# A slot schedule with two turned-back groups moved, one small result copied sooner, and two Vector steps written in fewer instructions

## The chip, the cores and the metric

The kernel runs on one core of a Trainium2 chip. The metric is the device time of one launch in microseconds; the time of a kernel is the median of its runs. Engines are named as the profile names them: PE is TensorE, PEld its weight loads, ACT is ScalarE, DVE is VectorE, POOL is GpSimd and SP is the queue that issues the transfers.

## The reference, cut to what matters

The model is two metaformer layers on an image batch of shape 8 x 96 x 128 x 128. Only the first layer's mixer and the first feed-forward matter here; the second layer is a convolution stage and another feed-forward. Cut down, the mixer is:

```python
feat, value = conv1x1(x, f_w, f_b), conv1x1(x, v_w, v_b)      # 4 heads of 24 channels, 4 quadrants of 64x64 tokens
ctr, value_centers = pool(feat), pool(value)                  # M = 4 centres for each head and quadrant
sim = sigmoid(beta + alpha * l2norm(ctr) @ l2norm(pts).T)     # 4 x 4096 for each head and quadrant
idx = argmax(sim, axis=1)                                     # each token keeps its best centre only, the first on a tie
sim = sim * (arange(M)[None, :, None] == idx[:, None, :])
agg = (sim @ value2 + value_centers) / (sum(sim, -1) + 1.0)
out = agg.T @ sim                                             # back to the tokens, then conv1x1 with proj_w
x = x + out
t = t + ffn(layernorm(t))                                     # hidden 384, operands rounded to an 8-bit float
```

## The kernel before, in words

The program has three phases, one after the other: `phase_a` (the mixer, the first feed-forward and the normalisation for the second layer, about 1,960 us), `phase_b` (the convolution over rows and columns) and `phase_c` (pointwise mix, gate and the second feed-forward). The change touches `phase_a` alone, and adds four columns to the constants.

**Steps and slots.** The image is cut into 32 quadrants of 4096 tokens (8 groups of 512 tokens, a group being `TPC` = 4 tiles of 128). `phase_a` is a software pipeline over quadrants. In step i each engine works on quadrant i (feed-forward), i+1 (result of the mixer, first norm of the feed-forward), i+2 (similarities) , i+3 (centres) and i+4 (turning the input). A step has nine slots, s = 0 to 8, written out by hand in the dictionaries at the top (`BIG_AT`, `FWD_AT`, `OUT_AT`, `COS_AT`, `SIM_AT`, ...); each of PE, ACT and DVE runs its own list through the slots, in program order, and waits on semaphores. POOL has its own order in a step (L1260 on), without slots.

What matters in a slot:

- The feed-forward of group s: PE `pe_hidden` in three parts j = 0, 1, 2 into two PSUM banks (L357), ACT `act_hidden` copies each (L370, tile `A_h`), DVE `dve_hidden` adds the bias and rounds (three L378, then one L382). ACT may run at most two groups ahead of DVE. PE `pe_q8` turns the next group's input (L267), ACT `act_q8` copies it (L305). `pe_y` (L297), `act_y` (L327) and `dve_y` (L249, L253) are group s-1.
- `big` (slots 0 to 3, two groups in each): features and dot products, PE L690, ACT L873 and L874; DVE `norms` reduces them (L1007), and after the fourth group of a half writes a seed (L1016) from which POOL computes inverse norms (`inverse_norms`, L1245 to L1258, result `A_rn`).
- `cosines` (slots 3 and 5, first DVE work of the slot) waits for `A_rn` of its half (L1025, L1029); then ACT takes the sigmoid (L956) and `similarity` (slots 4 and 6, last DVE work of the slot) finds the maximum (L1039), marks it (L1041), breaks ties (L1045, L1048, L1050) and writes the masked product (L1052). POOL `scaled_sim` (L1225) waits for that.
- The third stage of the output, x3: ACT `norm3` normalises a group (four L894; groups 0 to 3 in slots 7 and 8, groups 4 and 5 in slot 2 and 6 and 7 in slot 3 of the next step, `NORM3_LATE`). It waits for the shift that POOL `ln3` writes (L1207). PE `c_turn` turns a group back to channels (four L789 in a bank of the ring `back`), ACT `c_out` copies it out (L905), and SP stores a half when its four groups are there.
- The mixer's small chain for quadrant i+1: `gather_out` (slot 8), PE `sum_rows` (L729, L730), DVE `sum_out` (L1066), PE `values` (L738, first in slot 1, behind `keep_going`: matmuls on constants whose result nobody reads, L698), DVE `own_heads` (L1071, first in slot 1), PE `project` (slot 2), DVE `projected` (L1077, L1081), PE `out` (L781, slots 3 to 6).

PSUM banks are given out in rings: `front` with four banks, `back` with two. The order of the uses in a ring is the list written in the loop over slots, and a use waits for the reader of the use that had its bank before.

POOL's order in a step: the last half of `ln1` for i+3, `pool_norm` (L220, L229) of two groups, `ln3(p, 1)` for quadrant i-1 (p), `inverse_norms` of half 0, `pool_norm`, `inverse_norms` of half 1, `ln3(i, 0)`, `scaled_sim` of half 0, `ln2`, `centres`, `pool_norm`, `scaled_sim` of half 1, `ln2`, `pool_norm`, `ln1` for i+4.

Of the kernel before, what the change touches and what calls it, by code (L numbers as in the profile page):

```python
# [5 lines left out]
F32 = mybir.dt.float32  # L6
# [5 lines left out]
ALU = mybir.AluOpType  # L12
# [40 lines left out]
K_QUARTERS = K_ROWS + HM  # L53
K_W = K_QUARTERS + M

# [374 lines left out]
AGG_AT, SUM_AT, VAL_AT, PA_AT = 8, 0, 1, 2  # L430
KEEP_SIM, KEEP_VALUES = (8, 20), 12
NORM3_AT, NORM3_LATE = {7: (0, 1), 8: (2, 3)}, {2: (4, 5), 3: (6, 7)}


def phase_a(nc, consts, x, wf_t, wf, bf, wv_t, bv, wp_t, bp, alpha, beta, w1, b1, w2, b2, gamma, beta_ln, dw13, strip_dram, edge_dram, x2_dram, x3_dram):
# [4 lines left out]
    with ExitStack() as ctx:  # L440
# [3 lines left out]
        for s in range(FFN_SLOTS):  # L444
# [11 lines left out]
            if s == SUM_AT:  # L456
                front_uses.append(("sum", 0, 1, "summed", 0))
            if s == PA_AT:
# [3 lines left out]
            if s == AGG_AT:  # L462
# [190 lines left out]
        def _(pe):  # L653
# [138 lines left out]
            def body(i):  # L792
                q1, q2, q3, q4, p = i + 1, i + 2, i + 3, i + 4, i - 1
                for s in range(FFN_SLOTS):
# [27 lines left out]
                    if q1.real and s == SUM_AT:  # L822
                        sum_rows(i)
                    if q1.real and s == PA_AT:
# [142 lines left out]
        def _(dve):  # L967
# [63 lines left out]

            def similarity(q, h):
                n = NT // 2
                t, u = slice(h * n, (h + 1) * n), slice(h * n * HEADS, (h + 1) * n * HEADS)
                s3 = sim[:, t, :].rearrange("p t (h m) -> p (t h) m", m=M)
                e = eq[:, u, :]

                dve.wait_ge(ev["sig"], ev.at("sig", q, h))
                dve.tensor_reduce(mx[:, u], s3, AX_X, ALU.max).then_inc(ev["mx"], 1)  # L1039
                dve.wait_ge(ev["mx"], ev.at("mx", q, h))  # L1040
                dve.tensor_tensor(e, s3, mx[:, u].unsqueeze(2).to_broadcast([P, n * HEADS, M]),  # L1041
                                  ALU.is_equal).then_inc(ev["eq"], 1)

                dve.wait_ge(ev["eq"], ev.at("eq", q, h))
                dve.tensor_copy(taken[:, u, 0], e[:, :, 0]).then_inc(ev["tie"], 1)  # L1045
                for m in range(1, M - 1):
                    dve.wait_ge(ev["tie"], ev.at("tie", q, (M - 1) * h + m - 1))
                    dve.tensor_tensor(taken[:, u, m], taken[:, u, m - 1], e[:, :, m], ALU.max).then_inc(ev["tie"], 1)  # L1048
                dve.wait_ge(ev["tie"], ev.at("tie", q, (M - 1) * h + M - 2))
                dve.tensor_tensor(e[:, :, 1:M], e[:, :, 1:M], taken[:, u, :], ALU.is_gt).then_inc(ev["only"], 1)  # L1050
                dve.wait_ge(ev["only"], ev.at("only", q, h))
                dve.tensor_tensor(sim32[:, t, 0:HM], sim[:, t, :], e.rearrange("p (t h) m -> p t (h m)", h=HEADS),  # L1052
                                  ALU.mult).then_inc(ev["sim"], 1)

# [19 lines left out]
            def projected(q):  # L1074
# [45 lines left out]
            def body(i):  # L1120
# [3 lines left out]
                for s in range(FFN_SLOTS):  # L1124
# [851 lines left out]
```

## Time and profile before

| what | us |
|---|---|
| median of 3 runs (3660.05 to 3663.72) | 3662.53 |
| the profiled execution, its own time | 3659.49 |
| its span in the trace | 3657.6 |
| DVE busy over the span (88%) | 3218.4 |
| PE busy (82%) | 3017.4 |
| ACT busy (76%) | 2781.3 |
| POOL busy (47%) | 1728.9 |

The busy share of an engine is a mean over three phases with different limits, so it is read phase by phase. In a timeline of the trace a row gives the start, the time that the row's instructions cover, the engine and line, and in brackets how long the engine had stood idle before it and which instruction ended that. Rows that follow each other closely on one line are merged, with their count as x3.

### The profile page before, as it was taken

To read this page: it belongs to the slowest core of one execution; us is meant where nothing else is said; L and a number is where in the kernel's file an instruction comes from. 1 tells how busy PE (TensorE), PEld (TensorE's weight loads), DVE (VectorE), ACT (ScalarE), POOL (GpSimd) and SP (SyncE) were. 2 spreads that over 40 slices of the span, in tenths; PEclk is the share of its full clock that TensorE was granted. 3 is DMA by queue.
4 is the path that set the end of the run, shared out by engine and by line. 5 is a ranking of instruction groups with operands and counts; after the bars stand their busy time and mean duration, and the time that the engine had idled before them with its cause. 6 is when DMAs were issued, how large, how long until landed. Compare 5 with 4: busy or idle time off the path is not lost. (4 is left out here: it accounts for less than half of the span.)

```text
span 3657.6 us, 68122 instructions
## 1 busy us (share of the span) xinstructions
PE 3017.4 (82%) x21990; PEld 1910.0 (52%) x21990; DVE 3218.4 (88%) x8131; ACT 2781.3 (76%) x6274; POOL 1728.9 (47%) x2404
## 2 busy tenths in 40 slices
PE   6787888878787878887876799997888888888887
PEld 5565665656565656565654344443444444444444
DVE  4888889898989898989886699999899999999998
ACT  2577777777777877777778455554799999999998
POOL 3777777777787877787864000000222222222221
PEclk9999999899999999999987899999999999999999
DMA  3233323232323232323212888897676667666762
GB/s 68 53 89 74 91 71 88 71 88 70 88 71 88 71 88 71 88 71 88 71 56 69 212 238 234 236 280 212 172 199 188 181 185 200 184 184 193 199 177 83
DMA packets 696178, 478.92 MB, mean 131 GB/s; under 512 B 407217, under 2 KB 674422, under 8 KB 683830
## 3 DMA queue, kind: packets, MB, share of 16 engines
q1 hardware_dynamic: 695830, 474.58, 49.2%
q8 instruction: 182, 2.98, 0.3%
q14 instruction: 166, 1.36, 0.1%
HBM read 272.09 MB, written 201.92 MB: 130 GB/s over the span
## 5 line engine op out<-in xcount | busy, mean ns | idle before, releaser
L1891 POOL TENSOR_SCALAR C_var<-C_st 128x16 f32<-128x16 f32 x64 | 13.5, 211 | 1338.6 <-DVE C_st L178 1338.6
L1464 DVE SCALAR_TENSOR_TENSOR B_y<-B_mid,B_coefs,B_y 128x512 f32<-128x512 f32 x768 | 509.0, 750 | 3.2 <-ACT B_y L1429 3.2
L1395 PE MATMUL B_ps_row<-B_z,B_band 128*128 128x512 f32 x1152 | 499.1, 596 | 15.1 <-DMA B_band<-edge_scratch 15.1
L378 DVE TENSOR_SCALAR A_hq<-A_h,A_b 128x512 f16<-128x512 f16 x768 | 319.4, 456 | 176.5 <-ACT A_h L370 169.6
L370 ACT ACTIVATE A_h<-A_hid 128x512 f16<-128x512 f32 x768 | 428.3, 594 | 59.5 <-PE A_hid L357 57.1
L178 DVE BATCH_NORM_STATS2 A_st<-A_xT 128x6 f32<-128x192 f32 x1536 | 443.6, 349 | 29.3 <-ACT A_xT L861 16.0
L370 ACT ACTIVATE C_h<-C_hid 128x512 f16<-128x512 f32 x768 | 425.0, 589 | 22.9 <-PE C_hid L357 22.5
L1504 ACT ACTIVATE C_q<-C_xT,C_shift,C_rstd 128x96 fp8e5<-128x96 f32 x1024 | 392.6, 457 | 43.3 <-POOL C_shift L1898 43.2
L894 ACT ACTIVATE A_xc<-A_xT,A_shift,A_rstd 128x96 f32<-128x96 f32 x1024 | 379.3, 456 | 4.2 <-POOL A_shift L1207 4.0
L167 POOL TENSOR_TENSOR A_rstd<-A_var,A_expo 128x16 f32<-128x16 f32 x128 | 376.5, 2941 | 10.7
L1395 PEld LDWEIGHTS B_ps_row<-B_z,B_band 128*128 128x128 f32 x1152 | 218.8, 190 | 294.2 <-issue 287.8
L1738 PE MATMUL C_fbank<-C_y3q,C_pw 96*96 96x512 f32 x512 | 279.1, 627 | 77.7 <-DVE C_gated L1822 53.5
L357 PE MATMUL C_hid<-C_q8c,C_w 96*128 96x512 bf16 x768 | 259.3, 385 | 86.7 <-ACT C_h L370 83.4
L1420 ACT ACTIVATE B_mid<-B_ps_row,B_row_bias 128x512 f32<-128x512 f32 x192 | 130.4, 689 | 250.4 <-DVE B_y L1464 184.2
L297 PE MATMUL A_bbank<-A_w,A_hq 128*128 128x96 f16 x3072 | 192.6, 218 | 136.1 <-DVE A_hq L382 77.3
L357 PE MATMUL A_hid<-A_q8c,A_w 96*128 96x512 bf16 x768 | 267.3, 402 | 41.9 <-ACT A_h L370 39.5
L690 PEld LDWEIGHTS A_fbank<-A_big_w,A_xq 97*128 97x128 f32 x2048 | 275.9, 201 | 44.2 <-DVE A_pabd L1081 26.5
L690 PE MATMUL A_fbank<-A_big_w,A_xq 97*128 97x112 f32 x2048 | 282.2, 284 | 19.0 <-DVE A_pabd L1081 17.4
L378 DVE TENSOR_SCALAR C_hq<-C_h,C_b 128x512 f16<-128x512 f16 x768 | 243.7, 348 | 49.0 <-ACT C_h L370 38.9
L781 PE MATMUL A_fbank<-A_pabd,A_simT 128*128 128x384 f32 x512 | 244.0, 608 | 33.6 <-DVE A_xT L1088 33.6
L297 PEld LDWEIGHTS A_bbank<-A_w,A_hq 128*128 128x128 f16 x3072 | 165.5, 105 | 191.5 <-DVE A_hq L382 114.5
L305 ACT ACTIVATE A_q8c<-A_bbank 96x512 bf16<-96x512 f32 x256 | 149.3, 583 | 107.9 <-PE A_bbank L267 106.6
(167 smaller groups left out, 7248.7 us busy)
## 6 DMA issues: line engine op xcount, KB each, us to landing
A_xq<-in_x SPq DMA_DIRECT2D x32, 1536.0 KB, 8.9
x_scratch<-A_xT SPq DMA_DIRECT2D x64, 768.0 KB, 3.2
x_scratch<-A_x3h SPq DMA_DIRECT2D x64, 768.0 KB, 5.4
B_z<-x_scratch SPq DMA_DIRECT2D x96, 512.0 KB
y_scratch<-B_y SPq DMA_DIRECT2D x96, 512.0 KB, 3.6
C_x3q<-x_scratch SPq DMA_DIRECT2D x32, 1536.0 KB, 9.1
C_xT<-x_scratch SPq DMA_DIRECT2D x64, 768.0 KB, 16.6
C_y3q<-y_scratch SPq DMA_DIRECT2D x31, 1536.0 KB, 15.6
```

The source lines that it names most:

```text
L167: m = pool.tensor_tensor(rstd[:, o:o + n], var[:], expo[:, 0:n], ALU.pow)
L178: return dve.bn_stats(st[:, n:n + 2, :].rearrange("p t s -> p (t s)"), x[:, n * C:(n + 2) * C].rearrange("p (t c) -> p c t", t=2))
L297: m = pe.matmul(bank[:, t * C:(t + 1) * C], self.hq[:, b, s:s + P], self.w["w2"][:, j, :], start=(j == 0), stop=(j == NJ - 1))
L357: pe.matmul(self.hid2[n % 2][:], self.w["w1"][:, j * P:(j + 1) * P], self.q8c[:, k % 2, :], start=True, stop=True).then_inc(ev["hidden"], 1)
L370: act.activation(self.h16[:, k % 2, j * CH:(j + 1) * CH], self.hid2[n % 2][:], ACT.Copy).then_inc(ev["h16"], 1)
L378: r = dve.tensor_scalar(self.hq[:, b, s], self.h16[:, b, s], self.w["b1"][:, j:j + 1], 0.0, ALU.add, ALU.max)
L690: m = pe.matmul(bank[:, t * BIGN:(t + 1) * BIGN], xq[q.buf(NX)][:, n * P:(n + 1) * P], big_w[:, :], start=True, stop=True)
L894: m = act.activation(xc3[:, k // 4, t % (NT // 2), :], xT[u.buf(NB)][:, t * C:(t + 1) * C], ACT.Identity, scale=rstd3[:, t:t + 1], bias=sh ...
L1395: m = pe.matmul(bank(c, h), band[c.buf(NB)][:, d, :], z[c.buf(NB)][:, half(h), d:d + W], start=(d == 0), stop=(d == 2))
L1464: dve.scalar_tensor_tensor(y, mid[c.buf(2)][:, half(h), t:t + W], coefs[:, c.n, 3 + t:4 + t], y, ALU.mult, ALU.add).then_inc(ev["sums"], 1)
L1504: m = act.activation(self.q8[:, t, :], x[:, t * C:(t + 1) * C], ACT.Identity, scale=self.rstd[:, t:t + 1], bias=self.shift[:, t:t + 1], sa ...
L1738: pe.matmul(rows(front.bank("pw", k)[0:C, 0:CH]), pw[:], flipped(y3q[q.buf(2)], k), start=True, stop=True).then_inc(ev["pw_full"], 1)
```

## The change

It does six things, all in `phase_a`:

1. `c_turn` and `c_out` of groups 2 and 3 of the previous quadrant move from slot 0 to slot 3.
2. `sum_rows` on PE moves from the end of slot 0 to a place ahead of the second `big` of slot 0, and its place in the `front` ring with it; `sum_out` on DVE moves from the end of slot 0 to right behind `dve_hidden`.
3. The matmuls nobody reads in front of `values` go from 12 to 3 (`KEEP_VALUES`).
4. The tie break uses the first mark itself, where it had been copied first (L1045), and keeps its running maxima in the same tile, whose rows are 9 elements long, not 4.
5. The masked product L1052 is written with its heads and centres as two dimensions, since the marks no longer lie together.
6. The projected block matrix is written by one instruction of 128 x 384 with a mask of own blocks, where there were four of 32 x 96.

```diff
-C_AT_BEFORE = {0: (2, 3), 4: (4, 5), 5: (6, 7)}
+C_AT_BEFORE = {3: (2, 3), 4: (4, 5), 5: (6, 7)}
...
-KEEP_SIM, KEEP_VALUES = (8, 20), 12
+KEEP_SIM, KEEP_VALUES = (8, 20), 3
...
-            front_uses += [("big", c, 2, "big", c) for c in BIG_AT.get(s, ())]
+            front_uses += [("big", c, 2, "big", c) for c in BIG_AT.get(s, ())[:1]]
+            if s == SUM_AT:
+                front_uses.append(("sum", 0, 1, "summed", 0))
+            front_uses += [("big", c, 2, "big", c) for c in BIG_AT.get(s, ())[1:]]
...
-        eq = sb("A_eq", [P, NT * HEADS, M], F32)
-        taken = sb("A_taken", [P, NT * HEADS, M - 1], F32)
+        eq = sb("A_eq", [P, NT * HEADS, M * (M - 2) + 1], F32)
...
                     if i.real and s < NK:
                         ff.pe_hidden(pe, i, s, 2)
+                    if q1.real and s == SUM_AT:
+                        sum_rows(i)
                     for c in bigs[1:]:
                         big(i, c)
...
-                dve.tensor_copy(taken[:, u, 0], e[:, :, 0]).then_inc(ev["tie"], 1)
                 for m in range(1, M - 1):
...
-                    dve.tensor_tensor(taken[:, u, m], taken[:, u, m - 1], e[:, :, m], ALU.max).then_inc(ev["tie"], 1)
...
+                    dve.tensor_tensor(eq[:, u, M * m], eq[:, u, M * (m - 1)], e[:, :, m], ALU.max).then_inc(ev["tie"], 1)
...
+                dve.tensor_tensor(e[:, :, 1:M], e[:, :, 1:M], eq[:, u, 0:M * (M - 2) + 1:M], ALU.is_gt).then_inc(ev["only"], 1)
...
-                for t in range(TPC):
-                    g = slice(32 * t, 32 * t + 32)
-                    m = dve.tensor_scalar(pabd[g, t * C:(t + 1) * C], s_pa[g, 0:C], rden[g, :], None, ALU.mult)
-                m.then_inc(ev["pabd"], 1)
+                dve.scalar_tensor_tensor(pabd[:].rearrange("p (t c) -> p t c", c=C),
+                                         s_pa[:, 0:C].unsqueeze(1).to_broadcast([P, TPC, C]), rden[:],
+                                         own_block.unsqueeze(2).to_broadcast([P, TPC, C]),
+                                         ALU.mult, ALU.mult).then_inc(ev["pabd"], 1)
...
                     if i.real and s < NK:
                         ff.dve_hidden(dve, i, s)
+                    if q1.real and s == SUM_AT:
+                        sum_out(q1)
```

## Rows read from the trace of the kernel before

**Rows 1.** The page, its first line.
```profile
span 3657.6 us, 68122 instructions
```
**Rows 2.** Busy time by windows, first phase: start:end, length, engines, clock, DMA.
```profile
300.00:1800.00 1500.00, 1221.21 (x12187) 910.83 (x12186) 1313.86 (x3684) 1153.37 (x2787) 1155.00 (x1670) 0.93 0.33 80
```
**Rows 3.** Line L1066 in 300 to 1800 us: durations, first and last start.
```profile
L1066 DVE COPY A_summed<-A_fbank x25: 162/165/167, 305.5 to 1751.2; 97x16 f32<-97x16 f32 x25
```
**Rows 4.** Waits in 300 to 1800 us: total us, times, longest.
```profile
DVE A_hq L378 <- ACT A_h L370: 122.4, 101, 2.7
...
DVE A_rn L1025 <- POOL A_rn L1258: 3.8, 10, 0.4
```
**Rows 5.** Timeline of DVE, slots 0 and 1 of one step.
```profile
1026.37 0.35 DVE L378 TENSOR_SCALAR A_hq<-A_h,A_b 128x512 f16<-128x512 f16 x1 [1.94 <-ACT A_h L370]
...
1030.12 1.19 DVE L378 TENSOR_SCALAR A_hq<-A_h,A_b 128x512 f16<-128x512 f16 x2 [1.14 <-ACT A_h L370]
```
**Rows 6.** Timeline of POOL, from the scaled similarities to the inverse norms.
```profile
1013.37 0.66 POOL L1225 TENSOR_TENSOR A_simr<-A_sim,A_rstd 128x256 f32<-128x256 f32 x1 [3.07 <-DVE A_sim L1052]
...
1035.86 0.22 POOL L1207 TENSOR_TENSOR A_shift<-A_less,A_rstd 128x16 f32<-128x16 f32 x1
...
1040.98 0.32 POOL L1258 TENSOR_TENSOR A_rn<-A_newton 128x64 f32<-128x64 f32 x1
```
**Rows 7.** Timeline of DVE, end of slot 2 and start of slot 3.
```profile
1039.64 1.30 DVE L1081 TENSOR_SCALAR A_pabd<-A_fbank,A_rden 32x96 f32<-32x96 f32 x4
1041.33 0.23 DVE L1025 TENSOR_TENSOR A_rn<-A_rn,A_guard 128x64 f32<-128x64 f32 x1 [0.39 <-POOL A_rn L1258]
```
**Rows 8.** Timeline of DVE, the tie break in slot 6, this step and the next.
```profile
1011.60 0.22 DVE L1045 COPY A_taken<-A_eq 128x64 f32<-128x64 f32 x1
1011.85 0.59 DVE L1048 TENSOR_TENSOR A_taken<-A_taken,A_eq 128x64 f32<-128x64 f32 x2
...
1072.74 0.42 DVE L1052 TENSOR_TENSOR A_sim<-A_sim,A_eq 128x256 f32<-128x256 f32 x1
```
**Rows 9.** Timeline of ACT, slot 0 (a pair of L905 and what follows), then slots 2 to 4.
```profile
1023.92 1.44 ACT L905 ACTIVATE A_x3h<-A_bbank,A_gb 96x512 f32<-96x512 f32 x2
1025.25 0.49 ACT L873 ACTIVATE A_sq<-A_fbank 128x384 f32<-128x384 f32 x1
...
1036.12 2.97 ACT L894 ACTIVATE A_xc<-A_xT,A_shift,A_rstd 128x96 f32<-128x96 f32 x8 [0.34 <-POOL A_shift L1207]
...
1042.18 0.49 ACT L873 ACTIVATE A_sq<-A_fbank 128x384 f32<-128x384 f32 x1 [0.43 <-PE A_fbank L690]
...
1043.08 2.96 ACT L894 ACTIVATE A_xc<-A_xT,A_shift,A_rstd 128x96 f32<-128x96 f32 x8
...
1050.37 0.60 ACT L370 ACTIVATE A_h<-A_hid 128x512 f16<-128x512 f32 x1 [1.06 <-PE A_hid L357]
```
**Rows 10.** Timeline of PE: matmuls on constants, later its waits in slot 4.
```profile
1026.06 2.11 PE L698 MATMUL A_fbank<-A_w,A_idb 96*128 96x384 bf16 x12
...
1040.38 0.39 PE L357 MATMUL A_hid<-A_q8c,A_w 96*128 96x512 bf16 x1 [1.27 <-ACT A_h L370]
...
1047.16 0.71 PE L789 MATMUL A_bbank<-A_cst,A_xc 128*96 128x128 f32 x4 [1.92 <-ACT A_q8c L305]
```
**Rows 11.** Line L1464, the nearest instruction of the new kind.
```profile
L1464 DVE SCALAR_TENSOR_TENSOR B_y<-B_mid,B_coefs,B_y x768: 744/749/756, 2046.2 to 2554.4; 128x512 f32<-128x512 f32 x192
```
**Rows 12.** Timeline of DVE, slot 4, in both steps.
```profile
1050.63 1.04 DVE L378 TENSOR_SCALAR A_hq<-A_h,A_b 128x512 f16<-128x512 f16 x3
...
1112.43 0.35 DVE L378 TENSOR_SCALAR A_hq<-A_h,A_b 128x512 f16<-128x512 f16 x1 [1.17 <-ACT A_h L370]
```
**Rows 13.** Timeline of ACT, slots 3 and 4 one step later.
```profile
1105.17 2.96 ACT L894 ACTIVATE A_xc<-A_xT,A_shift,A_rstd 128x96 f32<-128x96 f32 x8
...
1111.80 0.60 ACT L370 ACTIVATE A_h<-A_hid 128x512 f16<-128x512 f32 x1 [0.40 <-PE A_hid L357]
```
**Rows 14.** Busy time by windows, slot 4 of the same step.
```profile
1048.00:1054.00 6.00, 5.22 (x25) 3.58 (x26) 5.87 (x18) 2.69 (x5) 3.54 (x12) 0.50 0.58 104
```

More of the change, by code:

```diff
@@ L53 @@
 K_QUARTERS = K_ROWS + HM
-K_W = K_QUARTERS + M
+K_BLOCK = K_QUARTERS + M
+K_W = K_BLOCK + TPC
 class Events:
@@ L452, in phase_a @@
                 front_uses.append(("val", 0, 1, "aT4", 0))
-            front_uses += [("big", c, 2, "big", c) for c in BIG_AT.get(s, ())]
+            front_uses += [("big", c, 2, "big", c) for c in BIG_AT.get(s, ())[:1]]
+            if s == SUM_AT:
+                front_uses.append(("sum", 0, 1, "summed", 0))
+            front_uses += [("big", c, 2, "big", c) for c in BIG_AT.get(s, ())[1:]]
             front_uses += [("out", k, 1, "x1", k) for k in OUT_AT.get(s, ())]
             front_uses += [("fwd", k, 4, "xT", k) for k in FWD_AT.get(s, ())]
-            if s == SUM_AT:
-                front_uses.append(("sum", 0, 1, "summed", 0))
             if s == PA_AT:
@@ L472, in phase_a @@
                     c16=1, cw=1, cwc=1, big=NK, n2=NK, n2c=2, seed=2, rn_s=22, rn=2, guarded=2, cos=2, sig=2, mx=2, eq=2,
-                    tie=6, only=2, sim=2, simr=2, simT=2, side=1, sided=1, pool=1, agg=1, gathered=2, sum=1, summed=1, val=1,
+                    tie=2 * (M - 2), only=2, sim=2, simr=2, simT=2, side=1, sided=1, pool=1, agg=1, gathered=2, sum=1, summed=1, val=1,
                     rden=1, aT4=1, pa=1, pabd=1, bn3=NK,
@@ L495, in phase_a @@
         sel_quarters = cst[:, K_QUARTERS:K_QUARTERS + M]
+        own_block = cst[:, K_BLOCK:K_BLOCK + TPC]
         w_raw = sb("A_w_raw", [C, 2 * C], F32)
@@ L821, in body @@
                             fwd(i, k)
-                    if q1.real and s == SUM_AT:
-                        sum_rows(i)
                     if q1.real and s == PA_AT:
@@ L1035, in similarity @@
                 s3 = sim[:, t, :].rearrange("p t (h m) -> p (t h) m", m=M)
-                e = eq[:, u, :]
+                e = eq[:, u, 0:M]
                 dve.wait_ge(ev["sig"], ev.at("sig", q, h))
@@ L1044, in similarity @@
                 dve.wait_ge(ev["eq"], ev.at("eq", q, h))
-                dve.tensor_copy(taken[:, u, 0], e[:, :, 0]).then_inc(ev["tie"], 1)
                 for m in range(1, M - 1):
-                    dve.wait_ge(ev["tie"], ev.at("tie", q, (M - 1) * h + m - 1))
-                    dve.tensor_tensor(taken[:, u, m], taken[:, u, m - 1], e[:, :, m], ALU.max).then_inc(ev["tie"], 1)
-                dve.wait_ge(ev["tie"], ev.at("tie", q, (M - 1) * h + M - 2))
-                dve.tensor_tensor(e[:, :, 1:M], e[:, :, 1:M], taken[:, u, :], ALU.is_gt).then_inc(ev["only"], 1)
+                    if m > 1:
+                        dve.wait_ge(ev["tie"], ev.at("tie", q, (M - 2) * h + m - 2))
+                    dve.tensor_tensor(eq[:, u, M * m], eq[:, u, M * (m - 1)], e[:, :, m], ALU.max).then_inc(ev["tie"], 1)
+                dve.wait_ge(ev["tie"], ev.at("tie", q, (M - 2) * h + M - 3))
+                dve.tensor_tensor(e[:, :, 1:M], e[:, :, 1:M], eq[:, u, 0:M * (M - 2) + 1:M], ALU.is_gt).then_inc(ev["only"], 1)
                 dve.wait_ge(ev["only"], ev.at("only", q, h))
-                dve.tensor_tensor(sim32[:, t, 0:HM], sim[:, t, :], e.rearrange("p (t h) m -> p t (h m)", h=HEADS),
-                                  ALU.mult).then_inc(ev["sim"], 1)
+                dve.tensor_tensor(sim32[:, t, 0:HM].rearrange("p t (h m) -> p t h m", m=M),
+                                  sim[:, t, :].rearrange("p t (h m) -> p t h m", m=M),
+                                  e.rearrange("p (t h) m -> p t h m", h=HEADS), ALU.mult).then_inc(ev["sim"], 1)
             def gather_out(q):
@@ L1154, in body @@
                         gather_out(q2)
-                    if q1.real and s == SUM_AT:
-                        sum_out(q1)
                     if q3.real and s == MEAN_AT:
@@ L1945 @@
         consts[32 * t:32 * t + M, K_QUARTERS:K_QUARTERS + M] = np.eye(M, dtype=np.float32) / np.float32(2 * CH)
+    for t in range(TPC):
+        consts[32 * t:32 * t + 32, K_BLOCK + t] = 1
     consts[0:C, K_CEN:K_CEN + C] = np.eye(C, dtype=np.float32) - np.float32(1 / C)
```

## The prediction, made before the changed kernel ran

> **What bounds the kernel now.** I read the page first: the profiled execution has a span of 3657.6 us [rows 1]. The change touches only the first phase, so everything is read there. In the busy time by windows, 300 to 1800 us, DVE works 1313.9 of 1500 us (88%) and no other engine over 82% [rows 2]. So DVE looks like the bound, with 186 us left over. The period of a step is the spacing of a line that runs once in it: L1066 runs 25 times, first at 305.5, last at 1751.2, so (1751.2 - 305.5) / 24 = 60.24 us [rows 3]. The waits say what DVE lacks: 122.4 us are for ACT's copy of the hidden layer, 4.9 us a step, and only 3.8 us for POOL's inverse norms, but those ten times [rows 4]. The timeline puts the waits for ACT mostly into slots 0 and 1: 1.94 us before the last L378 of slot 0, 1.14 us in slot 1 [rows 5].
>
> The reader is to see a second thing, which no sum of waits shows. POOL gets the masked product of half 1 (slot 6) after having stood idle for 3.07 us, and from then on its rows follow each other without a gap: L1225 at 1013.37, the shift L1207 ends at 1036.08, the inverse norms end at 1041.30 [rows 6]. DVE reaches `cosines` at 1041.33 after a wait of 0.39 us for just that [rows 7]. From L1052's end (about 1013.3) to that end are 28.0 us, all of it POOL's own work. A step is therefore a ring of two arcs: POOL's 28.0 us, and DVE from `cosines` at 1041.33 to the end of L1052 in the next slot 6, 1072.74 + 0.42 = 1073.16 [rows 7, 8], or 31.83 us. Together 59.86; the mean of 60.24 has 0.4 us more, from steps in which DVE is the later one at the meeting point or waits in slot 4.
>
> **The change, part by part.**
>
> *Slots 0 and 1.* The moved groups cost ACT, from the start of a pair of L905 to what follows, 1025.25 - 1023.92 = 1.33 us [rows 9]. With them gone ACT reaches the last L370 of slot 0 sooner; I take DVE's 1.94 us wait down to 0.2. The constant matmuls take 2.11 us for 12, 0.18 each, so nine fewer free 1.6 us of PE [rows 10]; with the sums copied ahead of the two L1007, the turning of slot 1's input is no longer behind them, and I halve the 1.14 us. Together some 2.3 us a step of idle DVE go away. All of it lies between the two ends of POOL's arc.
>
> *The block matrix.* Four L1081 take 1.30 us together [rows 7]. The trace of before has no such instruction of 384 elements. The nearest, L1464, takes 749 ns for 512 [rows 11]; by elements alone 562 ns, and with nothing scaled 749 are the bounds from below and above. Taken as 0.6 us (nearer to the scaled one), it saves 0.7 us. It lies in slot 2, so also inside POOL's arc. The Vector Engine (DVE) Microarchitecture Reference of the Trainium skill, section "Points that are easy to get wrong", warns that this form runs at half rate with two SBUF sources that are not bf16; the trace disagrees, for L1464 has two such sources and its 512 elements would then need over 1.07 us against 749 ns measured. By that rule the saving would be 0.3 us, not 0.7, and would hide in the same place.
>
> *The tie break.* L1045 goes; it costs from start to start 1011.85 - 1011.60 = 0.25 us [rows 8], in both halves, 0.51 us a step. These lie in slots 4 and 6, on DVE's arc, where DVE has no gap, so they count in full. The wider rows of the marks and the third dimension of L1052 I take as free; above, a loss of 0.1 us on each of three instructions in two halves would take it all back, below, no gain seems open.
>
> *What POOL's arc does to the gains.* DVE has a gain of 2.3 + 0.7 = 3.0 us ahead of `cosines`, and it was already waiting 0.39 us there. POOL has not one instruction less, so the 3.0 us turn into a wait for A_rn of some 3 us. Nor can ACT pass: its norms of groups 4 and 5 wait for the shift (0.34 us now [rows 9]) and would wait about 2 us more. What is left of slots 0 to 2 is nothing, apart from the last two steps, in which POOL has less to do. There DVE waits in slots 0 and 1 as well, and I give them 2 us each, 4 us in all.
>
> *What slot 3 pays.* Behind that shift ACT works almost without a pause to the last L370 of slot 4: from 1036.12 to 1050.97, with gaps of 0.43 and 1.06 us [rows 9]. DVE starts its three L378 of slot 4 at 1050.63 and ends them at 1051.67, so the third starts at about 1051.32 [rows 12]. ACT is thus 0.35 us early. The moved pair puts 1.33 us into this stretch. The gap of 0.43 us closes (it was for a bank that DVE now frees earlier), so the norms of groups 6 and 7 start at 1043.08 + 1.33 - 0.43 = 1043.98. With TensorE at full clock the last L370 follows 1111.80 - 1105.17 = 6.63 us later [rows 13] and ends at 1051.2: no stall. In the step shown slot 4 ran at a granted clock of 0.50 [rows 14], 1.2 GHz, after PE had stood idle 1.92 us and more for ACT [rows 10]; there the distance is 1050.37 - 1043.08 = 7.29 us, 0.66 more. With the change PE is done with slots 0 to 2 some 2 us sooner and then stands before the same ACT: its 1.27 us of idle in slot 3 [rows 10] become about 3. So I expect the clock to be at its lower level in slot 3 in most steps. The pair, `big` and `pe_y` of that slot are then in ACT's way; in full that costs 1.5 us (their 3.1 us of PE work doubled, less what ACT's pair covers), and since a fall covers only part of the slot I take 0.7. In the step where this happened before, DVE waited 1.17 us in slot 4 [rows 12]. With 0.66 in six steps of ten for slot 4, and 0.1 that was early taken off, the stall is 0.7 + 0.4 + 0.1 = 1.2 us.
>
> *The sum.* 28.0 + 31.83 - 0.51 + 1.2 = 60.52 a step, against 60.24: +0.28 in 27 steady steps is +7.5 us, less 4 at the end, +3.5. The profiled execution took 3659.5 us, which gives 3663.0; the median of the runs is 3.0 above that execution, so I predict 3666 us. A kernel's measurement here can tell apart about 0.2%, 7.3 us.
>
> **The rivals.**
>
> *The clock holds.* If PE's idle time falls so that slots 3 and 4 run at 2.4 GHz, nothing stalls in slot 4 (0.1 us) and a step takes 59.4 us: 27 x -0.84 - 4 = -27, 3636 us. For it speaks that ACT's arithmetic closes at full clock; against it the longer idle stretch just before. The fewer constant matmuls lie in slot 1 and matter less.
>
> *Both slots slow, on the other side.* If the lower clock lasts through slots 3 and 4, the stall is 1.5 + 0.66 + 0.1, about 2.3 us, and a step takes 61.6 us: 27 x 1.36 - 4 = +33, 3695 us. It decides from a stall of 0.92 us on, for there 59.86 - 0.51 + stall passes 60.24.
>
> *DVE and POOL get into each other's way differently.* L1029 and the L378 behind it run longer beside POOL's work, so two engines that overlap elsewhere can move POOL's arc by 0.4 us either way: 11 us up or down, 3655 or 3677. SBUF — State Buffer of the Trainium skill, section "SBUF: two separate sides", says that certain DVE instructions and POOL share one port pair as an exclusive lock; by it the newton steps would run free while DVE waits, and the work of slot 1 would be in POOL's way instead. I expect a draw.
>
> *No arc at all.* Were POOL not the limit, the whole 2.3 + 0.7 + 0.5 = 3.5 us a step would count, 27 x 3.5 = 95 us, 3567 us. Against it stands the unbroken chain of POOL.
>
> **How the numbers follow.** The forecast, a stall of 0.8 to 1.6 us, has 0.45 and covers 3655 to 3677; of it 0.27 fall within 0.2%, 0.16 slower, 0.02 faster. The clock holds: 0.24, faster. Both slots slow: 0.20, slower. Contention: 0.08, of which 0.05 faster, 0.03 slower. No arc: 0.03, faster. Together faster 0.34, same 0.27, slower 0.39. The range reaches to the two main rivals, 3636 and 3692, a little short of the slow one, so about 0.2 stays outside; the likeliest one's own range is 3655 to 3677.
>
> **What would show it.** In the trace after: DVE's waits in slots 0 and 1 shrink to about 1 us; before L1025 of half 0 there is a wait of 2 to 3.5 us for A_rn in nearly every step (ten short ones before); ACT waits some 2 us more for the shift; one L1081 of about 0.6 us; no L1045; 1 to 2 us of waiting before an L378 in slot 4; granted clock below 0.93 in the first phase. The period by L1066 should be 60.1 to 60.9 us. The prediction is wrong if the distance from L1052 to the end of A_rn is not 27.6 to 28.4 us, if DVE has no wait before L1025, or if slot 4 has none.

## The result, and the profile after

The changed kernel took 3712.43 us, median of 4 runs (3709.01 to 3717.41), against 3661.29 us before. The ratio is 1.014, its 95% interval 1.0122 to 1.0158: slower by 51 us, outside the predicted range of 3636 to 3692 us. One run of one kernel below (two Newton steps in the changed kernel) took 8122.85 us, a slow run, and is left out of its median.

The first line of the page, then one row each of three views of the first phase, 300 to 1800 us (the row of the copied sums, the busy time by windows, the waits):

```profile
span 3707.2 us, 67386 instructions
```
```profile
L1071 DVE COPY A_summed<-A_fbank x25: 167/168/170, 310.9 to 1795.6; 97x16 f32<-97x16 f32 x25
```
```profile
300.00:1800.00 1500.00, 1196.48 (x11745) 909.93 (x11745) 1255.59 (x3467) 1133.39 (x2721) 1131.59 (x1623) 0.90 0.38 78
```
```profile
DVE A_hq L379 <- ACT A_h L371: 138.8, 133, 2.1
PE A_bbank L791 <- ACT A_q8c L306: 107.0, 48, 4.1
...
ACT A_xc L896 <- POOL A_shift L1212: 59.2, 19, 3.1
DVE A_rn L1027 <- POOL A_rn L1263: 55.7, 19, 2.9
```

The copied sums now stand on L1071. Their spacing is (1795.6 - 310.9) / 24 = 61.86 us a step, against 60.24 [rows 3]: 1.62 more, 38.9 us over the 24 steps. The first of them comes 5.4 us later than before. The start of the second phase is read from the instruction of [rows 11], now L1469, which first starts at 2096.4 instead of 2046.2: 50.2 us later, so 5.9 us are lost behind the 25th row, and all of the loss is in the first phase. Neither the 5.4 us at the start nor the 5.9 us at the end was in the prediction's sum. The mean granted clock went from 0.93 [rows 2] to 0.90.

What was expected in slots 0 to 2 is there. The timeline of VectorE, slots 0 to 3 and the last group of slot 4, of a usual step:

```profile
805.03 0.35 DVE L379 TENSOR_SCALAR A_hq<-A_h,A_b 128x512 f16<-128x512 f16 x1 [0.71 <-ACT A_h L371]
...
818.19 0.62 DVE L1084 SCALAR_TENSOR_TENSOR A_pabd<-A_fbank,A_rden,A_cst 128x384 f32<-128x384 f32 x1
821.74 0.23 DVE L1027 TENSOR_TENSOR A_rn<-A_rn,A_guard 128x64 f32<-128x64 f32 x1 [2.93 <-POOL A_rn L1263]
...
833.35 0.35 DVE L379 TENSOR_SCALAR A_hq<-A_h,A_b 128x512 f16<-128x512 f16 x1 [1.78 <-ACT A_h L371]
...
854.26 0.43 DVE L1056 TENSOR_TENSOR A_sim<-A_sim,A_eq 128x256 f32<-128x256 f32 x1
```

The 1.94 us of slot 0 [rows 5] are 0.71 (0.2 were predicted), the block matrix is one instruction of 0.62 us, and both gains stand in the wait of 2.93 us for A_rn. The price is before the last group of slot 4: 1.78 us, where I had taken 1.2.

The timeline of ScalarE, slots 2 to 4 of the same step:

```profile
816.63 2.97 ACT L896 ACTIVATE A_xc<-A_xT,A_shift,A_rstd 128x96 f32<-128x96 f32 x8 [3.12 <-POOL A_shift L1212]
...
821.23 1.42 ACT L907 ACTIVATE A_x3h<-A_bbank,A_gb 96x512 f32<-96x512 f32 x2
...
824.75 0.49 ACT L875 ACTIVATE A_sq<-A_fbank 128x384 f32<-128x384 f32 x1 [1.01 <-PE A_fbank L692]
825.13 0.22 ACT L876 ACTIVATE A_dots<-A_fbank 128x64 f32<-128x64 f32 x1
825.71 0.49 ACT L328 ACTIVATE A_y<-A_bbank 128x384 f16<-128x384 f32 x1 [0.36 <-PE A_bbank L298]
...
832.72 0.60 ACT L371 ACTIVATE A_h<-A_hid 128x512 f16<-128x512 f32 x1 [0.41 <-PE A_hid L358]
```

From the shift to the last hidden copy are 833.32 - 816.63 = 16.7 us, against 14.85 before (1036.12 to 1050.97 [rows 9]). The two waits for TensorE in slot 3, 1.01 and 0.36 us, have their reason in the next view, TensorE's timeline of slot 3:

```profile
815.81 0.60 PE L791 MATMUL A_bbank<-A_cst,A_xc 128*96 128x128 f32 x4
820.51 0.61 PE L791 MATMUL A_bbank<-A_cst,A_xc 128*96 128x128 f32 x4 [4.10 <-ACT A_q8c L306]
820.96 1.64 PE L692 MATMUL A_fbank<-A_big_w,A_xq 97*128 97x112 f32 x8
822.39 0.64 PE L358 MATMUL A_hid<-A_q8c,A_w 96*128 96x512 bf16 x1
822.82 1.89 PE L692 MATMUL A_fbank<-A_big_w,A_xq 97*128 97x112 f32 x8
```

After 4.10 us of idle, eight matmuls of `big` take 1.64 and 1.89 us; at full clock they take 1.04. The busy time by windows shows how far the lower level (1.2 GHz) reaches, over slot 3 and then over slot 4:

```profile
821.20:828.00 6.80, 6.80 (x33) 5.53 (x32) 6.09 (x12) 5.43 (x15) 4.42 (x8) 0.50 0.57 118
828.10:834.00 5.90, 4.22 (x38) 2.96 (x36) 4.05 (x14) 5.19 (x11) 3.55 (x12) 1.00 1.15 166
```

POOL's arc is longer too. Its timeline:

```profile
793.26 0.67 POOL L1230 TENSOR_TENSOR A_simr<-A_sim,A_rstd 128x256 f32<-128x256 f32 x1 [2.88 <-DVE A_sim L1056]
...
805.14 3.12 POOL L168 TENSOR_TENSOR A_rstd<-A_var,A_expo 128x16 f32<-128x16 f32 x1
...
813.11 3.19 POOL L1210 TENSOR_TENSOR A_rstd<-A_var,A_expo 128x16 f32<-128x16 f32 x1
816.38 0.22 POOL L1212 TENSOR_TENSOR A_shift<-A_less,A_rstd 128x16 f32<-128x16 f32 x1
...
821.39 0.32 POOL L1263 TENSOR_TENSOR A_rn<-A_newton 128x64 f32<-128x64 f32 x1
```

The masked product of this step (L1056) ends at 793.19, A_rn at 821.71: 28.52 us. VectorE's arc runs from 821.74 to 854.26 + 0.43 = 854.69, 32.95 us. With 0.03 between them they make 61.5 us.

Last, what I had not foreseen at all. In 300 to 1800 us five of the 25 steps contain 14 to 17 us at the lower clock, from the end of slot 8 into slot 2; before, none does. The busy time by windows for one, and the waits in VectorE's timeline of that step:

```profile
551.70:568.80 17.10, 17.05 (x87) 14.76 (x88) 9.88 (x29) 9.81 (x23) 15.31 (x21) 0.50 0.09 37
```
```profile
556.85 0.35 DVE L379 TENSOR_SCALAR A_hq<-A_h,A_b 128x512 f16<-128x512 f16 x1 [1.71 <-ACT A_h L371]
...
561.28 1.19 DVE L379 TENSOR_SCALAR A_hq<-A_h,A_b 128x512 f16<-128x512 f16 x2 [1.37 <-ACT A_h L371]
563.83 0.35 DVE L379 TENSOR_SCALAR A_hq<-A_h,A_b 128x512 f16<-128x512 f16 x1 [1.36 <-ACT A_h L371]
...
586.34 0.35 DVE L379 TENSOR_SCALAR A_hq<-A_h,A_b 128x512 f16<-128x512 f16 x1 [2.13 <-ACT A_h L371]
```

TensorE is busy for 17.05 of 17.10 us at a granted clock of 0.50. Matmuls are then so slow that VectorE waits for ScalarE's copies of their results in slots 0 to 2 and no longer for A_rn. This step has 63.9 us. Only the two stretches of 17 us lie in such a step; the steps with the three of 13.7 us take 61.3 us, and some of the lengthening stands in the step before a stretch (62.7 to 63.4 us). Counted over all 24 steps, what goes beyond 61.43 us each is 10.6 us.

### The profile page after: what moved, and what is told of

Read it like the earlier page. It is cut to its first block and busy times, and to the rows that moved or that the text cites. A ratio compares the mean times of both kernels' runs of the same rounds, so it can differ in the third digit from the quotient of the medians.

```text
span 3707.2 us, 67386 instructions
## 1 busy us (share of the span) xinstructions
PE 3025.6 (82%) x21702; PEld 1937.9 (52%) x21702; DVE 3185.3 (86%) x7971; ACT 2789.4 (75%) x6274; POOL 1730.8 (47%) x2404
## 5 line engine op out<-in xcount | busy, mean ns | idle before, releaser
L1469 DVE SCALAR_TENSOR_TENSOR B_y<-B_mid,B_coefs,B_y 128x512 f32<-128x512 f32 x768 | 509.0, 746 | 3.2 <-ACT B_y L1434 3.2
L379 DVE TENSOR_SCALAR A_hq<-A_h,A_b 128x512 f16<-128x512 f16 x768 | 311.1, 441 | 208.0 <-ACT A_h L371 199.9
L692 PEld LDWEIGHTS A_fbank<-A_big_w,A_xq 97*128 97x128 f32 x2048 | 327.5, 233 | 28.1 <-issue 4.1
L692 PE MATMUL A_fbank<-A_big_w,A_xq 97*128 97x112 f32 x2048 | 332.2, 318 | 4.9 <-DVE A_big_w L1173 2.5
L358 PE MATMUL A_hid<-A_q8c,A_w 96*128 96x512 bf16 x768 | 280.9, 421 | 10.8 <-ACT A_h L371 7.7
L783 PE MATMUL A_fbank<-A_pabd,A_simT 128*128 128x384 f32 x512 | 253.6, 629 | 30.7 <-DVE A_xT L1093 30.5
L791 PE MATMUL A_bbank<-A_cst,A_xc 128*96 128x128 f32 x1024 | 156.5, 287 | 142.7 <-ACT A_q8c L306 133.4
```

What stands on the lines that cost most here:

```text
L358: pe.matmul(self.hid2[n % 2][:], self.w["w1"][:, j * P:(j + 1) * P], self.q8c[:, k % 2, :], start=True, stop=True).then_inc(ev["hidden"], 1)
L379: r = dve.tensor_scalar(self.hq[:, b, s], self.h16[:, b, s], self.w["b1"][:, j:j + 1], 0.0, ALU.add, ALU.max)
L692: m = pe.matmul(bank[:, t * BIGN:(t + 1) * BIGN], xq[q.buf(NX)][:, n * P:(n + 1) * P], big_w[:, :], start=True, stop=True)
L1469: dve.scalar_tensor_tensor(y, mid[c.buf(2)][:, half(h), t:t + W], coefs[:, c.n, 3 + t:4 + t], y, ALU.mult, ALU.add).then_inc(ev["sums"], 1)
```

## The experiments

"Long stretches" are stretches of over 10 us at the lower clock that begin at the turn of a step, counted in 300 to 1800 us (about 25 steps). Ratios are against the kernel before on the same chip; its medians were 3659.3 to 3663.1 us there, so a difference of less than some 4 us between two kernels below says nothing. Counts of stretches and lengths of steps come from one profiled execution each.

**One part alone.** The move alone, on the kernel before:

```diff
-C_AT_BEFORE = {0: (2, 3), 4: (4, 5), 5: (6, 7)}
+C_AT_BEFORE = {3: (2, 3), 4: (4, 5), 5: (6, 7)}
```


> The kernel before with groups 2 and 3 turned back in slot 3 instead of slot 0, and nothing else. Theory (two arcs: GpSimd fixes when the cosines of half 0 may start, and what is added on ScalarE behind the shift delays slot 4): the freed time in slots 0 and 1 turns into a wait before the cosines, the last hidden copy of slot 4 comes 1.7 us late as in the changed kernel, so a period of 61.2 to 62 us against 60.24 and 3690 to 3710 us in all. Rival (the loss comes from the fewer constant matmuls and a lower clock): no change, 3655 to 3668 us, and no wait over 1.5 us in slot 4.

Measured: 3709.85 us (four runs, 3697 to 3740), ratio 1.0145 (1.0099 to 1.0191), at the upper end of what the theory said. All but the move (the same line turned back in the changed kernel):

> The changed kernel with groups 2 and 3 back in slot 0. Theory: nothing is added behind the shift, slot 4 has no wait or a short one, the tie break's 0.5 us counts in full and GpSimd's arc is 28.0 to 28.5 us: a period of 59.4 to 59.9 us, 3640 to 3655 us. Rival (fewer constant matmuls or the new instructions cost the time): as slow as the changed kernel, 3700 us or more.

Measured: 3636.97 us, ratio 0.9938 (0.9923 to 0.9953), the best version that computes the whole reference. The three instruction edits alone (tie break, masked product, block matrix):

> The kernel before with the shorter tie break, the masked product and the block matrix in one instruction, and nothing else. Theory: 0.51 us a step from the tie break counts, the 0.7 us of the block matrix end in the wait for GpSimd: a period of 59.6 to 59.9 us, 3644 to 3656 us. Rival (all 1.2 us count): 58.9 to 59.1 us, 3625 to 3632 us. Second rival (the wider rows of the marks cost what the copy saved): 3655 to 3662 us.

Measured: 3641.9 us, ratio 0.9947 (0.9932 to 0.9961). So the move costs 75 us in the changed kernel, 3712.43 - 3636.97, and 48 us in the one before, 3709.85 - 3661.83. The edits of instructions give 20 of the 25 us that the rest brings (the kernel before had 3661.83 us beside them). Both theories named the right cause, with times at least 2 to 3 us too high. In the version without the move the wait for A_rn is as the ring says; the waits in 300 to 1800 us, and the row of the sums:

```profile
DVE A_rn L1027 <- POOL A_rn L1263: 32.1, 25, 1.4
```
```profile
L1071 DVE COPY A_summed<-A_fbank x26: 167/168/170, 308.1 to 1796.2; 97x16 f32<-97x16 f32 x26
```

(1796.2 - 308.1) / 25 = 59.52 us a step, with POOL's arc at 28.07 us and nothing waiting in slot 4. My ring without a stall, 59.86 - 0.51 = 59.35, is 0.17 off.

**Fewer constants.** The changed kernel with `KEEP_VALUES` 12 again:

> The changed kernel with 12 constant matmuls ahead of the values again. Theory: the common period of 61.4 us stays (GpSimd's arc and slot 4 are as they were), but the few steps of 62.7 and 63.9 us, with a stretch of 13 to 17 us at the lower clock, may go: 3695 to 3706 us, with the constants a little in the way in slot 1 but before the wait for GpSimd. Rival (the constants are the cause): back to 3655 to 3670 us.

Measured: 3730.46 us, ratio 1.0174 (1.0146 to 1.0202), 18 us above the changed kernel; 11 long stretches against 5. Neither forecast holds. Twelve constants in slot 1 did not keep the long stretches away. That they are only more work while the clock is low is my reading; the runs of this kernel scatter from 3713 to 3735 us, and no run isolates it.

**Other slots for the groups.** `C_AT_BEFORE = {2: ...}` and `{1: ...}` in the changed kernel:

> The changed kernel with groups 2 and 3 turned back in slot 2, ahead of ScalarE's wait for the shift (3.1 us there in the changed kernel). Theory (what is added behind the shift costs, what is added ahead of it is free): the wait for the shift shrinks by 1.3 us, slot 4 is on time, period 59.3 to 59.9 us, 3633 to 3650 us, level with or below the kernel that has them in slot 0. Rival (any move out of slot 0 lets the clock fall for long, and that is the cost): 3690 us or more.

> The changed kernel with groups 2 and 3 turned back in slot 1. Theory: as in slot 2, with 1.3 us of ScalarE's work back in slot 1, so the wait of VectorE in slot 1 is longer and the wait before the cosines shorter by as much: 3633 to 3650 us. Rival (the clock): 3690 us or more.

Measured: slot 2 3688.95 us, ratio 1.0084 (1.0068 to 1.0101), 11 long stretches; slot 1 3654.64 us, 0.9985 (0.9975 to 0.9994), 6 of them, each of 10.2 us. The theory fell for both; the rival of the clock holds for slot 2, within 1 us, and not for slot 1. So the move loses much ahead of the load that I priced: taking the groups out of slot 0 costs 52 us (3688.95 - 3636.97) though nothing is put behind the shift. In slot 1 they cost 18 us.

**Which ring.** Two Newton steps for three; the inverse norms are less exact, and POOL has 1.49 us less to do ahead of A_rn. In the changed kernel and in the one before:

```diff
-                for t in range(3):
+                for t in range(2):
```


> The changed kernel with two Newton steps instead of three for the inverse norms, so the inverse norms are less exact: 1.36 us less of GpSimd's work inside its arc (four rows of 0.24 to 0.32 us with their gaps). Theory: VectorE waits 2.9 us before the cosines, so all 1.36 us a step come off, some 35 us in all, 3670 to 3685 us. Rival (ScalarE in slot 4 or the clock sets the period by itself): no more than 10 us off.

> The kernel before with two Newton steps instead of three, inverse norms less exact. Theory: there VectorE meets GpSimd almost level (waits of 0.39 us in ten of 25 steps), so only 0.2 to 0.4 us of the 1.36 us come off: 3650 to 3660 us. Rival (GpSimd's arc is a full limit there as well): 35 us off, 3625 us.

Measured: 3716.36 us in the changed kernel (three runs), ratio 1.0149 (1.0132 to 1.0166), and 3652.65 before, 0.9978 (0.9968 to 0.9987). The first expectation, -35 us, fell and its rival holds; the second, 3650 to 3660 us, holds. VectorE's timeline shows where the 1.5 us went:

```profile
818.63 0.22 DVE L1027 TENSOR_TENSOR A_rn<-A_rn,A_guard 128x64 f32<-128x64 f32 x1 [1.46 <-POOL A_rn L1263]
822.48 0.35 DVE L379 TENSOR_SCALAR A_hq<-A_h,A_b 128x512 f16<-128x512 f16 x1 [0.97 <-ACT A_h L371]
...
832.06 0.35 DVE L379 TENSOR_SCALAR A_hq<-A_h,A_b 128x512 f16<-128x512 f16 x1 [1.98 <-ACT A_h L371]
```

The wait for A_rn halves, and waits for ScalarE in slots 3 and 4 take it over. So the ring that sets the changed kernel's period is not the one through A_rn. It runs from the masked product over POOL to the shift (793.19 to 816.60, 23.4 us), over ScalarE behind it to the last copy of slot 4 (16.7 us), and over VectorE to the next masked product (833.35 to 854.69, 21.3 us). These make 61.5 us as well; A_rn has slack inside it. In the version without the move it is the other way round:

> The change without the moved groups, with two Newton steps for the inverse norms where there are three: the inverse norms are less exact, POOL's work ahead of A_rn is 1.49 us less. Theory (in this version POOL's work from the masked product to A_rn sets the period, VectorE waits 1.43 us for it): the wait falls to under 0.3 us and a step from 59.4 to about 58.0 us, 27 x -1.4 = -38, about 3599 us. Rival (the ring over the shift and ScalarE's work behind it sets the period, as it did in the changed kernel): VectorE waits for ScalarE in slot 4 in its place and the time stays within 10 us of 3637.

Measured: 3621.54 us, ratio 0.989 (0.9874 to 0.9907). Its usual step is 58.1 us and VectorE no longer waits for A_rn, as the theory says; the mean is (1769.3 - 300.8) / 25 = 58.74, for two steps with a 17 us stretch take 63 us (10 us together) and some others 59 to 60. The time fell by 15 us, not by 38, which is neither the theory's time nor the rival's.

**POOL's order.** Inverse norms ahead of the shift, `NORM3_LATE` one slot later, groups in slot 0:

```diff
-                if p.real:
-                    ln3(p, 1)
...
                     if q2.real:
                         inverse_norms(q2, h)
...
+                    if p.real and h == 0:
+                        ln3(p, 1)
```


> The change without the moved groups, and on POOL the inverse norms of half 0 stand ahead of the shift ln3(p, 1), with ScalarE's norms of groups 4 to 7 one slot later (slots 3 and 4). Theory (POOL's work between the masked product and A_rn sets the period of the version without the move, where VectorE waits 1.43 us for A_rn): the 4.5 us of the shift leave the way to A_rn, that wait goes, and if nothing else waits a step takes 59.4 - 1.4 = 58.0 us, 27 x -1.4 = -38, about 3599 us. Rival (ScalarE's work behind the shift sets it): sixteen norms, 5.9 us, now all stand in slots 3 and 4 behind a shift that comes 5 us later; VectorE loses 1.5 to 2 us there and the step stays at 59 to 60 us, 3625 to 3655 us.

Measured: 3717.95 us, ratio 1.0154 (1.0139 to 1.0169). The theory fell, and the rival's time was too low as well: the wait for A_rn is gone, but many steps run at the lower clock in three places and take 62 to 64 us, and POOL now waits 148.2 us for the masked product (up to 8.0 at a time). This order costs 81 us against 3636.97. The run changes two things, POOL's order and the slot of ScalarE's norms, and does not say how much each costs.

**Constants against the lower clock.** 20 matmuls on constants in slot 3, between the turnings of groups 2 and 3, where TensorE was idle for 4.10 us:

```diff
+                            if k == 3 and i.real and q2.real:
+                                bank_free(front, i, "big", 6)
+                                keep_going(front.bank("big", 6), 20)
                             c_turn(i, p, k)
```


> The changed kernel plus 20 matmuls on constants in slot 3 between the turnings of groups 2 and 3, where TensorE stands idle for 4.10 us. Theory (the stall in slot 4 comes from slot 3 running at the lower clock behind that idle stretch): the granted clock of slot 3 rises to 1.0, the two big of it take 1.04 us each and not 1.64 and 1.89, the wait before the last L379 of slot 4 falls from 1.78 to 0.3 us or less, and a step takes 61.4 - 1.4 = 60.0 us in the usual case: 27 x -1.4 = -38, about 3675 us. Rival (ScalarE's amount of work behind the shift alone makes the stall, whatever the clock): the wait stays at 1.5 us or more and the time at 3705 to 3720 us.

Measured: 3712.89 us, ratio 1.0145 (1.0128 to 1.0162). The time says rival, the trace does not quite. TensorE's timeline shows the full clock, with the second line of `big` as the measure:

```profile
820.42 3.42 PE L700 MATMUL A_fbank<-A_w,A_idb 96*128 96x384 bf16 x20
...
825.22 1.04 PE L692 MATMUL A_fbank<-A_big_w,A_xq 97*128 97x112 f32 x8
```

In 13 of 24 steps the wait in slot 4 is now 0.7 us or less, where it was 1.78, and 11 of these take 60.2 to 61.1 us from one cosines to the next. So the lower clock in slot 3 makes more than 1 us of the stall. But ten steps now have a long stretch, with waits of 2.4 to 3.2 us in slot 3 and 1.6 to 2.3 us in slot 4, and the gain is gone. Constants in slot 0, four ahead of each `big` there, in the changed kernel and in the version with the groups in slot 2:

> The changed kernel plus four matmuls on constants ahead of each of the two big of slot 0, 8 x 0.18 = 1.4 us of TensorE. Theory (what the two groups did in slot 0 was to keep TensorE from running long at its lower level): the steps that now begin 14 to 17 us at the lower level (six of 27, 62.7 and 63.9 us long) become usual ones of 61.4 us: 3 x -2.5 + 3 x -1.4 = -12, about 3700 us. Rival (more columns while the clock is low only lengthen TensorE's work): such steps stay or become more, and the time is 3715 to 3730 us.

> The version with the two groups in slot 2 (3689 us), plus the same eight matmuls on constants in slot 0. In that version some 13 steps of 27 begin with 13.7 us at the lower level and take about 61.4 us, the others 59.9. Theory (work in slot 0 prevents those): most steps take 59.9 us, 10 x -1.5 = -15, about 3674 us or less. Rival (it lengthens them): 3695 to 3710 us.

Measured: 3764.9 us, ratio 1.0273 (1.0234 to 1.0312), where 15 steps have a long stretch and 64.9 us is the usual step; and 3688.38 us, 1.0075 (1.0057 to 1.0092), no change. In the first the theory fell; the rival had the direction and too small a size (3715 to 3730 us). In the second neither forecast holds.

**The old work of slot 0, engine by engine.** Eight turnings on TensorE ahead of the first `big` of slot 0; two copies on ScalarE into spare tiles; both:

```diff
+                if i.real and c == 0:
+                    for _ in range(8):
+                        pe.transpose(bank[0:C, 0:P], ident[:, 0:C], ident)
...
+                    if s == 0 and i.real and p.real:
+                        for b in range(2):
+                            act.activation(spare[b][:].rearrange("c (t p) -> c t p", p=P),
+                                           ident[0:C, :].unsqueeze(1).to_broadcast([C, TPC, P]), ACT.Identity,
+                                           scale=gb[:, 0:1], bias=gb[:, 1:2])
```


> The changed kernel plus eight turnings of 128x96 on TensorE ahead of the first big of slot 0, whose results nobody reads: TensorE has its old work in slot 0, ScalarE has not. Theory (TensorE's two turned groups kept its clock from staying low): the long stretches go away, about 3700 us. Rival (as with the matmuls on constants in slot 0, more work for TensorE while its clock is low only lengthens those steps): nearly every step becomes a long one of 64 to 65 us, 3740 to 3770 us.

> The changed kernel plus two copies of 96x512 on ScalarE in slot 0, at the place that the pair had, into spare tiles: ScalarE has its old work in slot 0, TensorE has not. Theory (it was ScalarE's pause in slot 0 that let TensorE get its work in order without long stretches at the lower level): the long stretches of 13.7 and 17.1 us go away, which leaves the usual step of 61.4 us: 3 x -2.5 + 3 x -1.4 = -12, about 3700 us. Rival (ScalarE is in the way in slot 0): DVE waits 1.9 us again there, which the wait for A_rn hides in usual steps, and the long stretches stay: 3712 us or more.

> The changed kernel plus both: eight turnings on TensorE and two copies on ScalarE in slot 0. Slot 0 is then as in the kernel without the move, and only the load in slot 3 differs. Theory (what the changed kernel loses is the load behind the shift, plus long stretches that come from slot 0): the time is that of the run with copies in slot 3 alone, within 10 us. Rival (the long stretches come from the shape of slot 3, not of slot 0): the time stays at 3712 us or above, and the six long stretches stay.

Measured: turnings 3680.78 us, ratio 1.0054 (1.0039 to 1.0069); copies 3713.94, 1.0151 (1.0134 to 1.0167); both 3686.39, 1.0068 (1.0053 to 1.0083). Useless work on TensorE made the kernel 32 us faster, 19 us beyond what its theory said. One long stretch is left of five, and the wait for A_rn is 1.4 us, not 2.9. ScalarE's copies gain nothing, as the rival said. With both, neither forecast holds: not the time of the run with copies in slot 3 alone (below), nor 3712 us.

The long stretches are the smaller part of that. In the 24 steps of 300 to 1800 us the turnings gain 24 us, and the stretches had cost 10.6. Two more things changed. POOL's arc is 28.07 us in the usual step and not 28.52, which 24 steps make 11 us. And slot 4 waits 1.42 us in the mean and not 1.81, which makes 9; the three overlap a little. The wait in slot 4 was 1.5 to 2.1 us in every step of the changed kernel; now it changes from step to step with the clock of slot 3. Two steps of the kernel with turnings, the windows of slot 3 and the waits in slot 4:

```profile
380.70:387.50 6.80, 6.80 (x32) 5.56 (x32) 5.92 (x12) 5.38 (x15) 4.40 (x8) 0.50 0.57 119
503.60:510.30 6.70, 4.36 (x38) 3.11 (x37) 6.53 (x14) 6.70 (x20) 4.32 (x8) 1.00 0.65 136
```
```profile
392.88 0.35 DVE L379 TENSOR_SCALAR A_hq<-A_h,A_b 128x512 f16<-128x512 f16 x1 [1.64 <-ACT A_h L371]
...
513.39 0.35 DVE L379 TENSOR_SCALAR A_hq<-A_h,A_b 128x512 f16<-128x512 f16 x1 [0.57 <-ACT A_h L371]
```

A stretch still begins at the turn of some steps, but it ends after 3.4 us; windows of the kernel with the turnings, the first mostly inside such a stretch, and what follows:

```profile
787.30:790.70 3.40, 3.40 (x19) 2.81 (x19) 1.16 (x6) 1.75 (x4) 3.01 (x5) 0.57 0.24 92
790.70:804.40 13.70, 12.74 (x172) 10.88 (x170) 10.79 (x27) 11.52 (x33) 12.64 (x19) 1.00 0.01 2
```

Then the load of slot 3 alone: the two copies at s == 3 in the version without the move.

> The change without the moved groups (3637 us), plus two copies of 96x512 on ScalarE in slot 3, at the place of the moved pair, into spare tiles that nobody reads: the load behind the shift alone, with slot 0 as it was. Theory (ScalarE's work behind the shift is too long for slot 4): the last L379 of slot 4 waits 1.5 to 2.1 us, a step goes from 59.4 to about 61.0 us, 27 x 1.6 = +43, about 3680 us. Rival (the lengthening comes from slot 0 having lost its pair): slot 4 waits under 0.5 us and the time stays at 3637 to 3650 us.

Measured: 3651.09 us, ratio 0.9981 (0.9972 to 0.999). That is 14 us above 3636.97, not 43: slot 4 waits 0.7 us at most, and the time is just past the rival's 3637 to 3650. ScalarE's time in slot 3 is the smaller part of what the load there costs. The copies here wait for nobody; the real pair needs TensorE's turnings, which stand behind ScalarE's copy of the next input. The turnings in slot 0 and the constants in slot 3 together:

> The changed kernel plus eight turnings on TensorE in slot 0 (which gave 3681 us) plus 20 matmuls on constants in slot 3 (which shortened the usual step to 60.2 to 60.5 us but made the long stretches at the lower clock more frequent). Theory (two separate losses, each of TensorE's clock: long stretches from slot 0, and the lower level in slot 3): both go, long stretches stay away, the wait in slot 4 falls under 0.7 us, a step takes 59.9 to 60.5 us, about 3681 - 27 x 0.9 = 3657 us. Rival (the constants in slot 3 bring the long stretches back whatever slot 0 does): 3690 to 3715 us.

Measured: 3689.07 us, ratio 1.0071 (1.0056 to 1.0086). No long stretch is left, yet a usual step is 61.5 us, with up to 2.17 us of waiting in slot 4: the lower clock now falls behind slot 3 (21.2 us after the copied sums, for 6.8 us). Neither theory had that.

## Why the prediction was wrong

- **POOL's arc and where the gains go: right, its size in part by luck.** "The 3.0 us turn into a wait for A_rn of some 3 us": 2.93 measured, ScalarE's wait for the shift 3.12. VectorE's waits for ScalarE in slots 0 and 1 did not shrink to about 1 us; four of them add up to 3.0 us (4.3 in the step of rows 5). From the masked product to where VectorE is ready for A_rn are 25.6 us (793.19 to 818.81) against 27.6 before, so 2.0 us were gained and not 3.0; the 0.39 us of before and 0.5 us more on POOL fill the rest. The block matrix took 0.62 us (0.6 said); it reads one operand from PSUM, so the case of two SBUF sources that the prediction priced at 0.3 us did not arise. The tie break: L1052's pair and L1054 follow L1045 without a copy; with the move left out the period is within 0.2 us of the ring.
- **The stall of slot 4: mis-sized.** The term "0.7 + 0.4 + 0.1 = 1.2 us" measured 1.78 in the usual step. Its parts failed both ways. The 0.7 took only part of 1.5 us for slot 3, but the lower clock lasted there through both `big`, in a stretch of 6.8 us in every usual step. The 0.4 was for slot 4 at the lower clock in six steps of ten, for which one step was shown [rows 14]; it was so in 7 of 24 steps of the trace before, and after, slot 4 of the usual step ran at a granted clock of 1.00. What I had called the load of ScalarE, 1.33 us, is worth 14 us by itself; with the turnings on TensorE in the same place and the clock, slot 3's share is 44 us (3680.78 - 3636.97), or 49 us by the kernel that also has the copies in slot 0 (3686.39). A stall of 1.2 us in 27 steps is 32 us.
- **Contention, "I expect a draw": wrong.** POOL's arc is 28.52 us, not 28.0. That is also outside the 27.6 to 28.4 us that the prediction staked. The same arc is 28.07 us in the kernel with turnings in slot 0 and 28.08 in the version without the move, with the same instructions on POOL. In the changed kernel the rows of 2.90 us on POOL take 3.12 and 3.19. That VectorE's earlier work beside them is the cause was not tested by itself. The Trainium skill (SBUF — State Buffer, "SBUF: two separate sides") has certain VectorE instructions and POOL share a port as a lock; the trace agrees as far as it goes: the Newton rows behind 818.81, beside an idle VectorE, take 0.32 us (L1259), and the rows beside slots 0 and 1 are the longer ones. Before, beside a busy VectorE, two of these Newton rows were longer, though beside other work of VectorE (829.23 to 832.55 in the changed kernel) they keep their 0.32 us; POOL's timeline of before:

```profile
1036.76 0.52 POOL L1254 TENSOR_TENSOR A_newton<-A_newton,A_n2c 128x64 f32<-128x64 f32 x1
...
1038.52 0.54 POOL L1254 TENSOR_TENSOR A_newton<-A_newton,A_n2c 128x64 f32<-128x64 f32 x1
```

- **The failed step: "What is left of slots 0 to 2 is nothing".** I counted what the groups cost in slot 0 and not what TensorE's turnings did there. The sum put that at nothing; giving TensorE its turnings back recovers 32 us, giving ScalarE its copies back nothing. Of this, the five stretches of 14 to 17 us at 1.2 GHz make some 10 us; the rest is POOL's longer arc and the longer wait in slot 4, where the lower clock fell into slot 3 in every usual step. That the turnings in slot 0 do it is shown; why 8 turnings do this and 8 constants do the opposite is not, and the two differ in type, place and amount.
- **The sum.** Said 60.52 us a step; usual steps have 61.4 (28.5 + 32.9), of which +0.5 is POOL's arc and +0.4 VectorE's. The steps around the long stretches bring the mean to 61.86. The 4 us that I gave the end came as a loss of 5.9, and the start lost 5.4. The stall at which the time would be level is 60.24 - 59.35 = 0.89 us, not 0.92.
- **The rivals.** The ring through A_rn was taken for the one that decides. With the stall it is the ring over the shift, to which POOL's last 5 us do not belong; two Newton steps showed it. The rival "both slots slow", with 0.20, had a step of 61.6 us, near the 61.4 of the usual one, but that is luck: its stall of 2.3 us measured 1.78, slot 4 was not slow, and 0.5 us of POOL's arc, which it did not have, made up for it. No rival had the long stretches or a loss in slot 0.

## What to carry to other kernels

Work that an engine off the critical path does in a pause is not only a cost: ask what TensorE's granted clock does in the stretch that loses it, and try the removal alone. A gain ahead of a fixed chain becomes a wait; before putting load behind that chain, find which of its outputs has slack (here A_rn had, the shift had none). The granted clock of the stretch that you load matters as much: slot 3 at 1.2 GHz made more than 1 us of a stall of 1.78. Here the move was the whole loss, and leaving it out gives 3637 us.

## What the runs showed of the hardware

- With slot 3 at a granted clock of 0.50 the wait in slot 4 was 1.64 us, at 1.00 it was 0.57 us, in two steps of one kernel.
- TensorE stayed at a granted clock of 0.50 (1.2 GHz) for 17.10 us while busy, as the profile models it, for 17.05 us of it. In the kernel with turnings, at the same place of a step, a window of 3.40 us with 3.40 busy has a mean of 0.57, and the 13.70 us behind it have 1.00.
- Matmuls on bf16 constants in slot 0 raised the number of such stretches (5 to 15); eight f32 turnings in the same slot cut it to 1.
- Operations of 2.90 us on POOL took 3.12 and 3.19 us in the changed kernel, by its own timeline; the cause was not isolated.
- SCALAR_TENSOR_TENSOR, 128x384 in f32 with PSUM and SBUF sources: 617 ns.
